# 64 bytes ahead of one SBUF buffer: operands 64 bytes apart modulo 128

## What is computed

```
xn  = layernorm(x)
qkv = xn @ Wqkv + bqkv                      # 16 heads of 16
s   = q k^T / 4, kept where |i - j| <= 64   # a band of 129 tokens
att = softmax(s) v @ Wout + bout
logits = xn @ router_w + router_b           # 8 experts, the top 2 kept
gate   = softmax of the two kept logits
moe = sum over the two experts e of gate_e * (relu(xn @ w1_e + b1_e) @ w2_e + b2_e)   # 256 -> 1024 -> 256
out = x + att + moe
```

## Time and profile before

| | us |
|---|---|
| median of three timed runs | 959.34 |
| the profiled execution's own time | 958.15 |
| its span, first to last instruction | 956.4 |
| TensorE busy in it | 918.7 |
| VectorE busy | 816.5 |
| ScalarE busy | 738.7 |
| GpSimd busy | 498.6 |

### The profile page before, as it was taken

One profiled execution on the slowest core, in us unless ns is written; L12 is line 12 of the kernel. 1 busy time (PEld: TensorE's weight loads), 2 busy tenths in 40 slices (PEclk: granted clock), 3 DMA queues, 4 the chain that ended last, 5 costly groups with the idle time before them and its releaser, 6 DMA issues.

```text
span 956.4 us, 27577 instructions
## 1 busy us (share of the span) xinstructions
PE 918.7 (96%) x7684; PEld 892.8 (93%) x7684; DVE 816.5 (85%) x2173; ACT 738.7 (77%) x1983; POOL 498.6 (52%) x700
## 2 busy tenths in 40 slices
PE   5998899999999999999999999999999999999996
PEld 4887888899999999999899999999999999999996
DVE  6886899998888888888788888888888888888885
ACT  4555899899999999999967777666677777777773
POOL 5211023155555555555546666666666666666662
PEclk9999899999999999999999999999999999999999
DMA  4989423444454444444263222221222222222210
GB/s 143 357 302 328 124 67 116 117 128 137 136 136 137 136 136 136 135 140 133 61 198 50 35 39 41 38 43 28 35 38 40 44 44 44 35 40 41 34 17 1
DMA packets 69885, 95.34 MB, mean 100 GB/s; under 512 B 15566, under 2 KB 48977, under 8 KB 69713
## 3 DMA queue, kind: packets, MB, share of 16 engines
q1 hardware_dynamic: 52816, 77.97, 26.6%
q0 software_dynamic: 17024, 16.88, 11.1%
HBM read 62.91 MB, written 35.53 MB: 103 GB/s over the span
## 4 chain that ended last, share of the span: by engine, by line
PE 77%; DVE 11%; issue 5%; ACT 5%; POOL 1%; DMA 0%; DVEq 0%; SPq 0%; ACTq 0%; POOLq 0%
PE ps_experts L1597 23%; PE ps_experts L1581 23%; PE ps_attend L1201 9%; PE ps_attend L1185 6%; PE ps_project L508 4%; DVE weights_qkv L875 4%; DVE work L886 3%; PE ps_attend L1171 3%; ACT weights_qkv L1091 2%; PE ps_project L486 2%; PE ps_attend L1233 2%; ACT work L1104 1%; PE ps_experts L1568 1%; PE ps_project L475 1%; PE ps_attend L1210 1%
## 5 line engine op out<-in xcount | busy, mean ns | idle before, releaser
L1091 ACT ACTIVATE weights_qkv<-weights_qkv,low 128x256 f32<-128x256 f32 (+1 forms) x512 | 240.2, 480 | 1.0 <-DVE low L875 1.0
L1523 ACT ACTIVATE hid<-ps_experts,b_s 128x256 f32<-128x256 f32 x312 | 130.9, 473 | 136.8 <-PE ps_experts L1581 136.2
L1581 PE MATMUL ps_experts<-work,q_st 128*128 128x256 f32 x1872 | 231.1, 283 | 0.1
L1581 PEld LDWEIGHTS ps_experts<-work,q_st 128*128 128x128 f32 x1872 | 227.4, 192 | 0.3 <-issue 0.3
L1419 POOL DMA_INDIRECT out<-y,target x78 | 129.5, 1661 | 126.3 <-DVE y L1490 109.8
L886 DVE TENSOR_TENSOR work<-ps_attend,work 128x512 fp32r<-128x512 f32 (+1 forms) x256 | 158.3, 619 | 39.1 <-ACT work L1104 38.6
L1201 PE MATMUL ps_attend<-work,v_m 128*80 128x256 f32 (+7 forms) x1536 | 186.9, 271 | 2.1 <-DVE inv_t L899 1.6
L1597 PE MATMUL ps_experts<-v_m,work 128*128 128x256 f32 x624 | 179.4, 287 | 0.7 <-DVE split L1465 0.7
L1597 PE MATMUL ps_experts<-k_st,work 128*128 128x256 f32 x624 | 176.5, 283 | 0.0
L1597 PE MATMUL ps_experts<-v_m,split 128*128 128x256 f32 x624 | 176.5, 283 | 0.0
L1201 PEld LDWEIGHTS ps_attend<-work,v_m 128*80 128x80 f32 (+3 forms) x1536 | 170.3, 162 | 3.8 <-issue 3.8
(11 more groups left out here) (181 smaller groups left out, 1703.2 us busy)
## 6 DMA issues: line engine op xcount, KB each, us to landing
weights_qkv<-in_w SPq DMA_DIRECT2D x15, 1024.0 KB, 6.1
qk_hi<-weights_qkv SPq DMA_DIRECT2D x16, 512.0 KB, 5.1
qk_lo<-weights_qkv SPq DMA_DIRECT2D x16, 512.0 KB, 6.0
q_st<-qk_hi SPq DMA_DIRECT2D x128, 64.0 KB
k_st<-qk_hi SPq DMA_DIRECT2D x128, 64.0 KB
xn_rows<-weights_qkv SPq DMA_DIRECT2D x8, 512.0 KB, 5.1
k_st<-qk_lo SPq DMA_DIRECT2D x64, 64.0 KB
q_st<-qk_lo SPq DMA_DIRECT2D x64, 64.0 KB
```

The source lines that it names most:

```text
L1091: ins = act.activation(wt[:, ring, at_tile(i)], wt[:, ring, at_tile(i)], ACT.Exp, bias=low[:, ring, i:i + 1], scale=-1.0, accum_out=total[ ...
L1523: ins = act.activation(hid[:, n % 2, j], ps[:, bank_h[n], j * ROWS:(j + 1) * ROWS], ACT.Relu, bias=b1[:, ds(e * FC + 2 * n + j, 1)])
L1581: ins = pe.matmul(ps[:, bank_h[m // 2], m % 2 * ROWS:(m % 2 + 1) * ROWS], w[:, c, m * P:(m + 1) * P], xx[:, c, :], start=(k == 0), stop=(k ...
```

## The change

A tensor of 16 floats per partition, which nothing uses, is laid out between `k_st` and `work`. `work` then starts at 189504 = 1480 x 128 + 64, and `split` and all that lies behind it also start 64 bytes higher.

More of the change, by code:

```diff
@@ L1687, in build @@
         g.k_st = sb("k_st", [P, 2, GP, N], F32R)
+        sb("apart_work", [P, 16])
         g.work = sb("work", [P, 4 * (6 * P + P)], F32R)
```

## The result

| | before | after |
|---|---|---|
| median, us | 958.8 (4 runs, 957.32 to 959.48) | 937.06 (4 runs, 936.41 to 938.9) |
| the profiled execution's own time, us | 958.15 | 936.41 |
| its span, us | 956.4 | 934.7 |

The ratio is 0.9778, with a 95% interval of 0.9759 to 0.9797: 21.7 us less. The forecast was 959.3 us with a range of 955.6 to 963.0, and faster had a chance of 0.08.

The account below looks back on a forecast made before the run. TensorE's 120 ns between expert products was taken as the bound. The only term, 3744 products times a change of 0 ns, left 958.2 us, or 959.3 us on the scale of the medians, range 955.6 to 963.0.

Parts of the forecast that it names:

- What bounds the kernel: Expert stage, 485 to 938 us: TensorE busy 452.9 of 453.0 us, starting one 128x256 product every 120 ns.
- (a): Expert products (L1581, L1597; 3744) and attention products (L1201; 1536) whose operands now differ by 64 modulo 128; effect taken as zero.
- I take 0 ns and 1 ns on either side: Change per expert product, read from projection rows L486 and L508 at c=0 and c=1; 1 ns would be 3.7 us.
- As they do not advance in step, a fixed difference of start addresses does not keep them apart: Argument against the faster rival: stream and weight load read at different paces, so offset start addresses cannot separate them.
- The faster rival: 256-wide products: loads and stream collide at equal addresses modulo 128; gain 3 ns each, some 13.5 us (945.8); chance 0.07.
- The attention's share of up to 4.6 us: Part of the faster rival: 1536 products at L1201 gain up to 3 ns each, half held back by ScalarE.
- The bound of 13.3 ns a product: Expert products' excess above one column a cycle (106.7 ns); removing all of it would give 50 us and 909.
- Slower rivals: First, expert products' streams meet at 64 apart: likelier 4.7 us, 964.0, chance 0.05; second, late gathers into `work`: 972, chance 0.01.

Follow-up runs that it names:

- pad128: Against the kernel before: 128 bytes of padding ahead of `work` in place of 64; 955.39 us, ratio 0.9969.
- pad192: Against the kernel before: 192 bytes of padding ahead of `work` in place of 64; 946.72 us, ratio 0.9864.
- stay64: Against the kernel before: 64 bytes ahead of `q_st` and 64 more ahead of `work`, so `q_st`, `v_m`, `k_st` stand at 64 modulo 128; 943.56 us, ratio 0.9851.
- late0: Changed kernel with the third ring buffer of gathered rows, read only by transposes, back at 0 modulo 256; 947.33 us, ratio 0.9877 to the kernel before.
- second64: Against the kernel before: only `h_hi` (inside `work`), `split` and what lies behind moved 64 bytes up; median 955.02 us, ratio 0.9941.
- bench3: Third streams-only kernel, TensorE alone: all 64 offsets of the streamed operand, then the second layer's order; 113.3 ns at 112 bytes, 130 at 104.

## Why the prediction was wrong

- *What bounds the kernel*: right. TensorE fills the expert stage before and after, and the difference is in the distance between starts.
- *"So the sum has one term, (a): 3744 expert products times the change in the 120 ns"*: right, and the term is what came. 3744 x 6.6 ns is 24.7 us, of which 22.8 arrive in the 38 steps: the first block and the first products of each L1597 block are slower, and in the last step TensorE waits (two starts stand 1409 ns apart, 979 before), so that hardly anything of that step's share arrives.
- *"I take 0 ns and 1 ns on either side"*: this step failed. Measured: 6.6 ns. The reading of the rows was right for the projection: over all groups at L486 in the trace of before, the median of three products is 368.5 ns with c=0 and 367.0 with c=1. L92 and L85 also show no gain at 64 bytes, alternating or 512 columns wide. What failed is the step from there to the expert products. The projection changes its difference every three products and is wider, the expert layers keep one difference through 48 products of 256 columns. I named the difference in width and covered it with 1 ns, without a row for it. Whether the width of 272 alone would already take the gain away, no run shows.
- *"As they do not advance in step, a fixed difference of start addresses does not keep them apart"*: wrong in what it was used for. A stream of equal products settles in a repeating pattern, and the addresses have a part in which patterns are possible. The trace of before had a hint that I didn't see: its L1581 blocks had 120 ns from start to start to within 1 ns, while at L486 the distances behind a product of 272 columns lay mostly between 121 and 129 ns. A distance that repeats so closely is a rhythm, and a rhythm may have others beside it.
- *The faster rival*: right in its direction and its place (only in the 256-wide steady state), chance 0.07. Its reason, a collision at equal addresses modulo 128, is not what came: 128 bytes apart is not the same as 0 (L77, pad128), 192 bytes of padding gave 946.72 us and not 937 (pad192), and a collision itself was not measured. Its price of 3 ns was taken from the rate per column at 512 columns, which was no bound here: 113.3 ns lie below the 117 that it gave. The attention's share of up to 4.6 us doesn't show. The bound of 13.3 ns a product, with 909 us, held, but stood outside the range.
- *Slower rivals*: neither came. Something like the first exists, though: at 80 loaded columns 64 bytes cost 2.4 ns a product (L90, L91), and at 104 bytes the streams lose 10 ns.
- *The page of the Trainium skill (TensorE: Matmul & The Clock Gate)*: I weighed two of its statements and sided with the one that gave nothing. The formula N / 2.4 + 2.5 ns of "Back-to-back issue gap" gives 109 ns for an isolated matmul and says nothing of addresses; of the 11 ns between it and the trace, 6.6 came. That loading the next weights takes no read bandwidth from the running matmul ("Step-by-step: what each phase is for") is not tested by these runs, but what I drew from it, that the offset is worth nothing, is refuted: moving the loaded tile alone by 64 bytes, all other engines idle, takes a stream from 11.66 to 11.47 us (L82, and L80 of the same kernel).

The 64 bytes alone don't make the 937. stay64 has the same differences and 943.56 us, and late0 moves one operand outside the products and has 947.33.

What stays open is the mechanism in the chip. That the two reads of SBUF meet in the same part of the memory, and that one waits, would agree with a dependence on both addresses and on the time at which each read begins; no run here looks at the reads themselves. Open, too, is which entry brings L1581 to 113 in the kernel, as the streams at its pair of addresses never got there.

## What to carry to other kernels

In a stage in which TensorE never waits, measure the distance between starts, and if it is the same number everywhere and lies above one column a cycle (106.7 ns for 256 columns here), try a few paddings of one operand. Judge an offset by its blocks in the kernel itself, over several executions: what runs before a block takes part in it, and a later change of another buffer can lose part of the gain (late0 lost 10 us, second64 scattered over 9). A comparison of two rows in one trace should be carried over only to products of the same width in the same unbroken order; here it was not, and that cost the forecast.

## What the runs showed of the hardware that was not expected

- Streams of 128x256 float32r products with 128 loaded columns settle in repeating distances, with means of 113.3, 117.8 and 120.0 ns among them; at 113.3 the single distances are 113 and 114 ns, at 117.8 they are 117 to 119. Two of these rhythms can exist for the same addresses.
- The distance has no smooth dependence on the offset: 113.3 ns at 112 bytes, 130 ns at 104 bytes (bench3).
- With 192 or 128 streamed columns and 128 loaded ones the streams have 111 to 112 ns (10.86 us for 96 products of either width at 0, 10.88 at 64 bytes): here the number of streamed columns no longer sets the pace. That the load does agrees with the attention's products in the trace of before, where equal neighbours of 192 columns at L1201 stand 90 ns apart with 80 columns loaded and 114 with 128 (medians).
